# A fused gated-scan and Hadamard-FFN layer: W2 prepared behind the first gate and up products, a fourth butterfly stage on GpSimd, norms by pairs, new orders

## The reference

```python
def layer(x, Wi, Wf, Wg, Wo, gnorm_w, W1, W2, W3):           # x: 4 x 512 x 512, H = 2048
    a = layernorm(x)
    f, i, g = a @ Wf.T, a @ Wi.T, a @ Wg.T
    o = scan(o_t = sigmoid(f) * o_(t-1) + silu(i) * (1 - sigmoid(f)))   # over time
    o = o * rsqrt(mean(o*o) + eps) * gnorm_w * silu(g)
    x = x + layernorm(o @ Wo.T)
    z = layernorm(x)
    h = fwht(silu(z @ W1.T) * (z @ W3.T))                     # Walsh-Hadamard over 2048
    return x + layernorm(h @ W2.T)
```

## Time and profile before

| | us |
|---|---|
| median of 3 runs | 722.8 (721.26 to 724.37) |
| the profiled execution | 722.41 |
| its span, first to last instruction | 720.6 |
| mean granted TensorE clock | 0.983 |
| PE busy | 689.6 (96% of the span) |

### The profile page before, as it was taken

The page is one execution under the profiler, slowest core; times in us unless marked ns, Lnnn a source line. Parts: engine busy times, 40 slices in busy tenths (PEclk is TensorE's granted clock), DMA queues, the critical chain, the costliest instruction groups (busy, mean ns, idle before and its releaser), DMA issues.

```text
span 720.6 us, 11006 instructions
## 1 busy us (share of the span) xinstructions
PE 689.6 (96%) x4148; PEld 414.3 (57%) x4148; DVE 469.3 (65%) x782; ACT 290.4 (40%) x498; POOL 322.2 (45%) x268
## 2 busy tenths in 40 slices
PE   3979899999998999999999999999999999999996
PEld 2534344444443445865657767556577777867772
DVE  5989698988586766743468674547476553744554
ACT  4756865753553332324423332264133212221231
POOL 2969869737899752202425331107262212211222
PEclk9989989999998999999999999999999999999998
DMA  8943224457766348562343565404556462246102
GB/s 319 405 154 122 88 89 147 146 177 173 262 235 217 134 81 307 125 203 89 117 177 144 119 248 121 173 15 162 205 151 157 128 238 100 107 146 237 42 1 88
DMA packets 63717, 114.36 MB, mean 159 GB/s; under 512 B 38320, under 2 KB 42672, under 8 KB 59056
## 3 DMA queue, kind: packets, MB, share of 16 engines
q1 hardware_dynamic: 63664, 113.66, 47.5%
HBM read 81.92 MB, written 23.07 MB: 146 GB/s over the span
## 4 chain that ended last, share of the span: by engine, by line
PE 77%; POOL 9%; DVE 5%; DMA 3%; issue 2%; SPq 2%; ACT 1%; POOLq 0%; DVEq 0%; ACTq 0%
PE ps L633 24%; PE ps L634 24%; PE ps L635 24%; PE ps L795 1%; PE ps L796 1%; DVE ring L1135 1%; SPq L563 1%; POOL ring L1440 1%; POOL ring L1438 1%; POOL ring L1436 1%; DMA ring<-W13t 1%; POOL ring L1442 1%; DMA ring<-L_attn_Wf 1%; POOL rstd L1374 1%; POOL ot L1392 1%
## 5 line engine op out<-in xcount | busy, mean ns | idle before, releaser
L633 PE MATMUL ps<-xb,ring 128*128 128x256 f16 (+1 forms) x704 | 226.9, 322 | 1.5 <-DVE ring L1135 1.2
L635 PE MATMUL ps<-xb,ring 128*128 128x256 f16 (+1 forms) x704 | 227.0, 322 | 0.0
L634 PE MATMUL ps<-xb,ring 128*128 128x256 f16 (+1 forms) x704 | 227.0, 322 | 0.0
L633 PEld LDWEIGHTS ps<-xb,ring 128*128 128x128 f16 x704 | 69.2, 98 | 49.3 <-issue 3.9
L634 PEld LDWEIGHTS ps<-xb,ring 128*128 128x128 f16 x704 | 69.0, 98 | 46.6 <-issue 2.1
L635 PEld LDWEIGHTS ps<-xb,ring 128*128 128x128 f16 x704 | 69.1, 98 | 42.8 <-issue 1.1
L1374 POOL TENSOR_TENSOR rstd<-var,neg_half 128x1 f32<-128x1 f32 x64 | 40.3, 638 | 103.8 <-DVE var L1100 38.6
L1446 POOL TENSOR_TENSOR hsp<-sga,hsp 128x512 f16<-128x512 f32 x34 | 42.0, 1238 | 98.5 <-ACT hsp L1049 98.5
L634 PE MATMUL ps<-ring 128*128 128x256 f16 x288 | 78.5, 273 | 0.0
L635 PE MATMUL ps<-ring 128*128 128x256 f16 x288 | 78.5, 273 | 0.0
L633 PE MATMUL ps<-ring 128*128 128x256 f16 x288 | 78.5, 273 | 0.0
(11 more groups left out here) (200 smaller groups left out, 1304.6 us busy)
## 6 DMA issues: line engine op xcount, KB each, us to landing
ring<-w_comb SPq DMA_DIRECT2D x24, 1792.0 KB, 7.9
ring<-W13t SPq DMA_DIRECT2D x16, 512.0 KB, 11.4
ring<-W13t SPq DMA_DIRECT2D x8, 1024.0 KB, 6.6
w_comb<-ring SPq DMA_DIRECT2D x8, 1024.0 KB, 8.5
rows<-L_attn_hidden_states SPq DMA_DIRECT2D x16, 256.0 KB, 3.1
w2t<-W2t SPq DMA_DIRECT2D x8, 512.0 KB, 13.0
res<-L_attn_hidden_states SPq DMA_DIRECT2D x16, 256.0 KB, 4.0
x_rows<-res SPq DMA_DIRECT2D x16, 256.0 KB, 2.0
```

Of the source, the lines that this page charges most:

```text
L633: pe.matmul(dst, a_hi, b_hi, start=start, stop=False)
L634: pe.matmul(dst, a_hi, b_lo, start=False, stop=False)
L635: return pe.matmul(dst, a_lo, b_hi, start=False, stop=stop)
```

## The change

1. `H2` takes one matmul a half instead of two: POOL now does four butterfly stages (8 operations a unit, 64 in all) and not three (48). The result lies in `unit_raw`, and all units share one scratch tile, `x1r`. `neg_had` goes.
2. The queue of loads: Wo, the residual rows and the Hadamard matrix, then chunks 0 to 7 of W1 and W3, W2 units 0 to 3, chunks 8 to 15, and units 4 to 7.
3. `D.0.0` and all that follow stand behind `UP.0.15`. UP's results of batch 0 from chunk 2 on lie in the ring, in the places of weight chunks that have been stored.
4. The raw pairs of the weight sums have one place: `SL` of a pair waits for `SO` of the pair before.
5. `WN` squares two chunks in an instruction, 16 instructions of 1024 elements instead of 32 of 512. `WS` handles both scales together, and the bound of the hidden values is a step of its own (`HB`).
6. The loads `WL.1.1` and `WL.1.2` wait for the last `D` step of batch 0 and for all stores of sums.
7. New tables of order for all five engines.

```diff
-        def unit_tmp(m):
...
-        UNIT_TMP = ("x1r", "hsp", "sga", "x1r", "hsp", "ot0", "ot1", "x1r")
+        unit_tmp = x1r[:].rearrange("p s d -> p (s d)").rearrange("p (c d) -> p c d", d=UW)
...
-        def comb_raw(j):
-            return kb(56 if j % 2 else 32, 8).bitcast(F32).rearrange("p (c w k n) -> p c w k n", c=2, w=2, k=KC)
+        comb_raw = kb(60, 8).bitcast(F32).rearrange("p (c w k n) -> p c w k n", c=2, w=2, k=KC)
...
         def hid(b, c, part):
-            if early(b, c):
-                return xb[:, 1, part, c - 2]
+            if b == 0 and c >= 2:
+                return kb(32 + 2 * (c - 2) + part, 1)
...
             def load_raw_pair(j, _):
                 if j == 0:
-                    sp.wait_ge(up_mm, 2)
-                    sp.wait_ge(st_a[0], 32)
-                elif j == 1:
...
+                    sp.wait_ge(up_mm, 9)
+                    sp.wait_ge(st_a[0], 96)
+                    sp.wait_ge(st_a[1], 64)
                 else:
-                    sp.wait_ge(s_lo, 2 * j - 2)
...
+                    sp.wait_ge(s_lo, 2 * j)
...
-                    sp.wait_ge(up_mm, (13, 10, 16)[n])
-                    if n == 1:
-                        sp.wait_ge(s_lo, HC)
+                    sp.wait_ge(up_mm, HC)
+                    if n > 0:
+                        for i in range(2):
+                            sp.wait_ge(st_s[i], 16 * (HC // 4))
+                        sp.wait_ge(d_mm, HC)
...
-            for m in range(4):
-                load_unit(m)
-            sp.dma_start(had[:], hadamard).then_inc(ld_had, 16)
-            for m in range(4, UNITS):
-                load_unit(m)
             load_attention(3, w_o)
             for t in range(TC):
                 load_res(0, t)
-            for c in range(HC):
+            sp.dma_start(had[:], hadamard).then_inc(ld_had, 16)
+            for c in range(HC // 2):
                 load_pair(c)
+            for m in range(4):
+                load_unit(m)
+            for c in range(HC // 2, HC):
+                load_pair(c)
+            for m in range(4, UNITS):
+                load_unit(m)
...
-                pe.wait_ge(w2_fly, 6 * (m + 1))
-                low, high = (unit_tmp(m)[:, HC // 2 * s:HC // 2 * (s + 1), :].rearrange("p c d -> p (c d)")
-                             for s in range(2))
-                pe.matmul(bank("H2", m, h)[:], had[:], low, start=True, stop=False)
-                pe.matmul(bank("H2", m, h)[:], neg_had[:] if h else had[:], high, start=False, stop=True
-                          ).then_inc(h2_mm, 1)
+                pe.wait_ge(w2_fly, 8 * (m + 1))
+                chunks = unit_raw(m)[:, HC // 2 * h:HC // 2 * (h + 1), :].rearrange("p c d -> p (c d)")
+                pe.matmul(bank("H2", m, h)[:], had[:], chunks, start=True, stop=True).then_inc(h2_mm, 1)
...
-                if b == 0 and EARLY <= c < EARLY + 2:
-                    act.wait_ge(d_mm, c - EARLY + 1)
...
+                if b == 0 and c >= 2:
+                    act.wait_ge(st_a[(c - 2) // 4 % 2], 32 * ((c - 2) // 8 + 1))
```

More of the change, by code:

```diff
@@ L43 @@
[L43 to L47, removed]
@@ L419, in mixer_ffn_kernel @@
         ld_wc = [sem(f"ld_wc{i}") for i in range(SLOTS)]
-        ld_s = [sem(f"ld_s{i}") for i in range(2)]
         ga_mm, up_mm, sga_rdy, hid_rdy, hid_hi, hid_lo, d_mm, d_out = (sem(s) for s in (
@@ L470, in chunk @@
             return slice(c * P, (c + 1) * P)
-        def early(b, c):
-            return b == 0 and 2 <= c < EARLY
         def late(b, c):
@@ L767, in ws @@
                 wait_bank("WS", b, t)
-                pe.wait_ge(squared, max(squares_to["WN", c, 0] for c in range(HC)))
-                pe.matmul(bank("WS", b, t)[:, 0:2 * HC], ones[:], wn2[:].rearrange("p w c -> p (w c)"),
+                pe.wait_ge(squared, max(squares_to["WN", j, 0] for j in range(HC // 2)))
+                pe.matmul(bank("WS", b, t)[:, 0:HC], ones[:], wn2[:].rearrange("p w c -> p (w c)"),
                           start=True, stop=True).then_inc(w_norm, 1)
@@ L956, in gated @@
                     act.wait_ge(y_mm, TC * b)
-                if c == 0 and b == 1:
-                    act.wait_ge(h2_mm, 14)
                 if n == 0:
@@ L1236, in ws, with hidden_bound @@
                 settle()
+                exp = [exps[:, w:w + 1].bitcast(I32) for w in range(2)]
                 for w in range(2):
-                    exponent_scales(w_sum[:, w:w + 1], dve_chain, w_s[:, w:w + 1], w13_inv[:, w:w + 1], w_srdy)
-                    settle()
+                    dve.tensor_scalar(exp[w], w_sum[:, w:w + 1].bitcast(I32), 24, None, ALU.logical_shift_right
+                                      ).then_inc(dve_chain, 1)
+                settle()
+                settle()
+                for w in range(2):
+                    dve.tensor_scalar(exp[w], exp[w], float(F_LEAST), None, ALU.max).then_inc(dve_chain, 1)
+                settle()
+                settle()
+                for w in range(2):
+                    dve.tensor_scalar(w_s[:, w:w + 1].bitcast(I32), exp[w], -BIT, (127 + ROW_EXP) * BIT, ALU.mult, ALU.add
+                                      ).then_inc(w_srdy, 1)
+                for w in range(2):
+                    dve.tensor_scalar(w13_inv[:, w:w + 1].bitcast(I32), exp[w], BIT, (127 - ROW_EXP) * BIT,
+                                      ALU.mult, ALU.add).then_inc(dve_chain, 1)
+                settle()
+                settle()
+            def hidden_bound(b, t):
+                pairs = HC // 2
                 dve.wait_ge(ws_read, 1)
@@ L1275, in combine_u2 @@
                 if n == 0:
-                    for j in range(2):
-                        dve.wait_ge(st_s[j], 16 * (HC // 4))
+                    dve.wait_ge(d_mm, 13)
                 if n >= 2:
@@ L1433, in weight_sums @@
             def weight_sums(j, _):
-                pool.wait_ge(ld_s[j % 2], 16 * (j // 2 + 1))
-                a11, a12, a21, a22 = (quad(j, c, h) for c in range(2) for h in range(2))
+                pool.wait_ge(ld_s, 16 * (j + 1))
+                a11, a12, a21, a22 = quad(0, 0), quad(0, 1), quad(1, 0), quad(1, 1)
                 pool.tensor_tensor(a22, a21, a22, ALU.add).then_inc(sa_rdy, 1)
```

362 lines of the change are left out of this document (174 added, 188 removed).

## The result

| | before | after |
|---|---|---|
| median of the runs | 723.2 (721.26 to 724.37) | 712.63 (708.99 to 713.35) |
| span of the profiled execution | 720.6 | 710.2 |
| mean granted clock | 0.983 | 0.977 |
| PE busy, PE idle | 689.6, 31.0 | 677.2, 33.0 |

The account below looks back on a forecast made before the run. PE, busy 96% of the span, was taken to bound the kernel. The terms summed as 720.6 - 8.2 + 1.7 - 5.5 - 1.1 + 1 + 7 + 1 = 716.5 us of span, with 1.8 around it 718; range 707 to 728.

Parts of the forecast that it names:

- my own case: Whole kernel: the forecast itself, with PE waiting at the first GP of batch 1; 718 us (713 to 722), chance 43%.
- rival 1: Batch 1: the covers hold, PE waits neither at GP.1.0 nor at GP.1.2; 709 us (704 to 713), chance 25%.
- D's wait: D step waiting on GpSimd: its wait of 1.1 us goes, since D now has 50 steps of cover; -1.1 us.
- DVE's pace in the gate products: Batch 0's products: at 1.43 us a WT, DVE has UP.0.4 done at 134, when GA.0.7 wants it; +1 us.
- z transposes: At GP.1.0: UP.0.15 ahead on DVE makes z late; PE waits 4 us and pays 3 for the clock, +7.
- weights of GP.1.2: End of the weight sums: WL.1.1 brings the weights at 319, GP.1.2 wants them at about 322; +1 us taken.
- the whole direct gain: H2: 32 float32 matmuls become 16, 13.8 us less PE work, in full only if no new wait takes it back.
- The start: Ahead of the first Y: PE idles some 13 us, Y starts at about 70, first gate product at 97, 8.2 us earlier.
- MS in batch 1: MS, batch 1: GpSimd's sums done at about 211, PE gets there at 213; no wait, -5.5 us.
- Serial rounds: Weight sums, one place for raw pairs: eight rounds of 17 to 20 us end at about 302; +1 us.
- Rival 2: At GP.1.2: rounds of 20 us, deciding from about 18.5, make PE wait 13 us; 733 us (726 to 740), chance 20%.
- Rival 3: Gate products: at 1.7 us a WT or above, DVE makes PE wait 4 to 6 us; 725 (721 to 729), chance 12%.

Follow-up runs that it names:

- the table of four kernels: Against the kernel before (1): old order with half the H2 matmuls 721.04 us, 0.999; new order with each H2 matmul twice 719.82, 0.998; changed kernel 712.63, 0.985.
- the second run: The changed kernel again, unchanged, in a later series: 711.13 us, 0.986 (0.983 to 0.988) of the kernel before.

## Why the prediction was right, and where its sum was off

The forecast was right in direction and in most steps, but its size was off: 718 us against 712.6, a gain of 0.6% where 1.5% came. The time lies within the stated range of 707 to 728, just outside the 713 to 722 of my own case, and inside rival 1's 704 to 713. In span it is 716.5 against 710.2. Term by term:

| term | forecast | measured |
|---|---|---|
| first gate product earlier | -8.2 | 105.2 - 96.2 = -9.0 |
| more H2 behind it | +1.7 | 10 x 0.86 - 6.9 = +1.7 |
| MS and Y of batch 1 without wait and clock loss | -5.5 | full clock, no wait: -5.5 |
| D's wait | -1.1 | gone: -1.1 |
| DVE's pace in the gate products | +1 | 0 |
| z transposes | +7 | 2.1 + 1.7 = +3.8 |
| weights of GP.1.2 | +1 | 0 |
| sum | -4.1 | -10.1; by the spans -10.4 |

**H2.** Right. That it counts only if no wait takes it back is the step on which all hangs, as the table of four kernels shows. The prediction called it the whole direct gain, and that was right only in the new order.

**The start.** Right: PE idled 9.3 + 0.2 + 0.2 us for W2 and the first gate product started 0.8 us ahead of the forecast. I had expected 13 us of idle time, counted with MS; unit 4 came at 64 and PE did W2N in the gap. That ACT's path and the queue end together was right (GpSimd's last low part ended at 68.15, and MS started behind W2N.7 at 68.65), with WS as a third chain that I had not named. The clock behind the wait was near 0.5, as forecast, by the window from 64 to 74:

```profile
64.00:74.00 10.00, 9.52 (x51) 6.63 (x52) 5.32 (x21) 5.00 (x9) 9.54 (x8) 0.51 0.23 92
```

ACT's last step ahead of Y, after:

```profile
65.86 0.61 ACT L936 ACTIVATE ot<-sg 128x512 f16<-128x512 f32 x1
```

GpSimd's:

```profile
66.99 1.16 POOL L1383 TENSOR_TENSOR ot<-sg,ot 128x512 f16<-128x512 f32 x1
```

ACT was done at 66.5; the sum from the earlier trace rows gave 64 without and 68 with waits.

**MS in batch 1.** The term of -5.5 came out, and the times nearly too: GpSimd's last sum ended at 210.3 (211 was forecast) and MS started at 211.9 (213). GpSimd's row, then PE's:

```profile
209.06 1.26 POOL L1378 TENSOR_TENSOR osum<-osum,osq 128x512 f32<-128x512 f32 x1 [4.96 <-ACT osq L917]
...
211.89 0.95 PE L725 MATMUL ps<-ones,osum 128*128 128x1 f32 x8
```

But the reason was in part luck. I had added up GpSimd's work; it stood idle 5.0 us ahead of this sum, for a square that ACT makes, so its work was not what set the time. The margin was 1.6 us.

**DVE's pace.** The term of +1 was mis-sized. DVE's WT from 96.2 to 140, in the view that groups instructions (busy us, mean ns):

```profile
L1256 DVE SCALAR_TENSOR_TENSOR ring<-ring,w_s 128x512 f16<-128x512 f32 x20 | 25.2, 1294 | 0.8 <-ACT ring L971 0.8
```

They took 1.29 us on average where I had 1.43. (My 1.43 was from eleven in 15.7 us; the trace of the kernel before has 13 in 17.9 us up to 136, each 1.38, so the count was wrong and the pace nearly right.) The 13 of them between `UP.0.1` and `UP.0.4` took 14.2 us, 1.09 each, and `UP.0.4` was there at 131.1 + 0.7, where I had 134:

```profile
131.08 1.40 DVE L1334 SCALAR_TENSOR_TENSOR sga<-ps,up_c,sga 128x512 f32<-128x512 f32 x2
```

`GA.0.7`, 14 products and one H2 half behind 96.2, wanted it at 133.4. So this place had 1.6 us of slack: the danger was real, and my pace a little too slow. The Trainium skill, SBUF — State Buffer, "Who interferes with whom", has DVE with two SBUF inputs and GpSimd reading SBUF exclude each other; read strictly, that was 2.0 us a WT by the prediction's estimate. The trace does not agree with so strict a reading here: WT took 1.29 on average while GpSimd was busy 94% of the time, and three in a row took 3.24 us beside two butterflies:

```profile
120.28 3.24 DVE L1256 SCALAR_TENSOR_TENSOR ring<-ring,w_s 128x512 f16<-128x512 f32 x3 [0.79 <-ACT ring L971]
```

GpSimd in the same stretch:

```profile
119.03 3.29 POOL L1408 TENSOR_TENSOR w2t<-x1r 128x512 f32<-128x512 f32 x2
```

**z transposes.** The mechanism was there and its size was off: +3.8 and not +7. The step that failed is that `UP.0.15` on DVE alone sets the start. It does so for the first three statistics of z (DVE has `UP.0.15` at 230.2 and the first of them at 230.9), but not for the fourth. GpSimd's rows after, the first of `SA.4` and then `YN.1.3`:

```profile
230.11 1.27 POOL L1423 TENSOR_TENSOR ring<-ring 128x512 f32<-128x512 f32 x1 [0.48 <-DMA ring<-W13t]
...
235.38 1.27 POOL L1392 TENSOR_TENSOR res<-res,rows 128x512 f32<-128x512 f32 x1
```

DVE's fourth statistics:

```profile
236.68 0.69 DVE L1068 BATCH_NORM_STATS2 st<-res 128x6 f32<-128x512 f32 x1 [2.57 <-POOL res L1392]
```

GpSimd makes `SA.4`, which waits for its load, ahead of `YN.1.3`, and the fourth statistics wait for that. `SO.4`, which I had named too, follows on DVE and took 2.5 us, not the 4.5 of the earlier trace rows. So the last tile of z was there at 242.0, just as forecast, but by luck: a wait of 2.6 us that I did not have stood against 2.0 us too many for `SO.4`. The first transpose came at 242.7 (I had 244), the last landed at 264.5 (266 to 267), and D ended at 262.5 (263.5). The clock cost 1.7 us, not 3, and in the second run nothing.

**Serial rounds.** The mechanism and most numbers held; the term of +1 was 0. The eighth round ended with DVE's last split at 300.4, where I had about 302:

```profile
297.94 2.48 DVE L1262 SCALAR_TENSOR_TENSOR ring<-ring,w_s 128x1024 f16<-128x1024 f32 x2 [2.28 <-ACT ring L983]
```

`WL.1.1` was issued at 304.8, so some 4.4 us went to the store, for which I had taken 7.9. The transfer took about 8 us, and `GP.1.2` started at 318.3 without a wait: some 5 us of slack were left, where the prediction had 3. Rival 2 did not come up; that it would from 18.5 us a round on was not shown.

**The rivals.** The time lies between rival 1's 709 and my forecast: its covers held at `GP.1.2`, and at `GP.1.0` only half. Rival 3 is out too: PE has no wait for DVE in the gate products.

## What to carry to other kernels

Work taken off a bound engine counts only where the engine has no wait behind it that grows by as much: the same 16 matmuls were worth 0.1% in one order and 1.3% in the other. A wait named in the profile belongs to the last of several chains that may end together; before one is removed, look for when the others end, and after it, for what the next stage waits for. A wait of 9.3 us was worth nothing here.

## What the runs showed that was not expected

An added idle time can make the work behind it slower than what was saved: with half the matmuls in the old order the first gate product came 3.1 us later, with granted clocks of 0.73 (77 to 87) and 0.72 (87 to 105.2) where the kernel before has 1.00 and 0.81. And the same wait of 2 us at `GP.1.0` was followed by a clock of 0.78 in one execution of the kernel and by 1.00 in another. So a clock loss behind a short wait belongs into the range and not into the sum.
